# Where the maxima are transposed in the first attention: a bank of the maximum pass, ahead of the last value products

## The chip, the cores and the metric

The kernel runs on one core of a Trainium2 chip. The metric is device microseconds (us) from the first to the last instruction of the program, median of several runs. The engines of the core are TensorE (PE in the profile; its weight loads are PEld), VectorE (DVE), ScalarE (ACT), GpSimd (POOL) and SyncE (SP, which issues the DMAs here). Each executes its own list of instructions in order and waits on semaphores for the others. TensorE writes only to PSUM, which has eight banks of 512 float32 columns in 128 partitions.

## The reference

Two layers. The change is in the attention of the first one, which takes the first half of the time:

```python
b, s, d = x.shape                                  # 4, 1024, 256
q = jnp.einsum('bsd,hqd->bhsq', x, w_q)            # 16 heads of 64
k = jnp.einsum('bsd,hqd->bhsq', x, w_k)
v = jnp.einsum('bsd,hvd->bhsv', x, w_v)
scores = jnp.einsum('bhsq,bhtq->bhst', q, k)
masked = jnp.where(causal, -jnp.inf, scores)
weights = jax.nn.softmax(masked / jnp.sqrt(jnp.float32(dq)), axis=-1)
out = jnp.einsum('bhst,bhtv->bhsv', weights, v)
return jnp.einsum('bsf,df->bsd', cat, w_o)
...
x = x + _layernorm(_L0_attn_ref(_layernorm(x, axis=-1), ...), axis=-1)
x = x + _layernorm(_L0_ffn_ref(_layernorm(x, axis=-1), ...), axis=-1)   # a second attention and 8 experts, top 2
```

## The kernel before

`attention_one` works on pairs of heads: 8 pairs in each of 4 sequences, so 32 pairs. A pair goes through four steps of a pipeline, and in every step four pairs are at work: `n0` gets the first halves of its Q and K projections, `n1` the second halves, its V and its maximum pass, `n2` its scores, exponentials and value products, and `n3` its last value products, sums and normalisation.

A step has 12 slots (`n` = 0 to 11). Each slot is one unit of scores of `n2`, a block of 128 keys by up to 512 queries, for both heads `h`. The order inside a slot is written out by hand, for every engine in its own `step` function, and the engines meet through semaphores alone. The steps run in loops: an inner loop of two steps a turn (line 257), an outer loop over three sequences (line 265), and some steps written out at both ends.

- The **maximum pass** of `n1` (PE line 641) computes scores without a shift into three banks in turn, `MX[c % 3]`, 24 matmuls a pair. DVE takes the row maxima from them (lines 501 and 504), and its last instruction, line 507, writes `minus` (128 x 16), the negated maxima of both heads.
- The **turn**: PE transposes `minus` (line 726), DVE copies the result into `minusT` (line 527, function `turn`), and SP sends it by two DMAs into row 64 of `QS` (line 381). The semaphores are `minus_ready`, `turn_ready`, `turn_copied` and `minus_in`. The scores of that pair in the next step (lines 577 and 578, a product of 128 rows and one of 65 rows, the 65th holding the negated maxima) wait for `minus_in` at their first unit.
- The bank `PV` takes four things in turn: the second half of the Q projection (`qk(n1, p, 0, 1, PV)`, line 618, slot 0), V (line 626), the sums of the later half of the queries (line 605), and the transposed maxima. In the last step of a sequence (`wo` set) the output projection (line 651) uses it too, and ACT takes the rows out (`proj_copied`).
- **Slots 9, 10 and 11** of a step: in slot 9 PE projects the first half of K of `n0` into `PK`. In slot 10 ACT copies it out for both heads between its exponentials (line 407) and DVE computes the rounding rests, `split_k` (line 520). PE issues the value products of group 4 in slot 10 (`output`, line 595), which wait for the masks of POOL (line 330). In slot 11 there are only the last scores of the step.
- DVE also does the additions of head 0 for the row sums (line 291, `late_add`) and POOL those of head 1.

Below, the end of slot 10 to the start of slot 0 is called a boundary; there are 32, one for each pair, numbered from 0.

Of the kernel before, what the change touches and what calls it, by code (L numbers as in the profile page):

```python
# [16 lines left out]
P = 128  # L17
# [5 lines left out]
ST_N = S // P  # L23
# [163 lines left out]
def attention_one(nc, hold, w_pair, w_out, inv_rows):  # L187
# [5 lines left out]
    with ExitStack() as ctx:  # L193
# [278 lines left out]
        def _(dve):  # L472
# [50 lines left out]
            def turn(n1):  # L523
                dve.wait_ge(s["turn_ready"], n1 + 1)

                dve.wait_ge(s["minus_in"], n1 * 32 + 1)
                dve.tensor_copy(minusT[:, :], PV[0:2 * ST_N, 0:P]).then_inc(s["turn_copied"], 1)

            def step(n0, n1, n2, n3, p, begins=False, wo=None):
                for n in range(NU):  # L530
# [6 lines left out]
                    one_max()  # L537
                    for h in range(2):
                        if n1 is not None and n == Q1_SLOT:
                            split_q(n1, p, 1, h)  # L540
                        if n1 is not None and n == K1_SLOT + 1:
                            split_k(n1, p, 1, h)
                        if n0 is not None and n == Q0_SLOT + 1:
                            split_q(n0, 1 - p, 0, h)
                        if n0 is not None and n == K0_SLOT + 1:
                            split_k(n0, 1 - p, 0, h)
                        one_max()
                    while maxima:
                        one_max()
                    if n1 is not None and n == TURN1_SLOT:  # L550
                        turn(n1)
# [8 lines left out]
        def _(pe):  # L560
# [69 lines left out]
            def maximum(n1, p, c):  # L630
# [8 lines left out]
                pe.wait_ge(s["max_used"], n1 * NMAX + c + 1)  # L639
                bank = MX[c % MAX_BANKS1]  # L640
# [14 lines left out]
            def step(n0, n1, n2, n3, p, begins=False, wo=None):  # L655
                for n in range(NU):
# [6 lines left out]
                    if n1 is not None and n == Q1_SLOT:  # L663

                        pe.wait_ge(s["turn_copied"], n1 + 1)
                        qk(n1, p, 0, 1, PV)
# [33 lines left out]
                    one_max()  # L700
                    if n3 is not None and n == 0:
                        output(n3, p, GROUPS - 1)
# [9 lines left out]
                    if n3 is not None and n == SUM_SLOT[1]:  # L712
# [3 lines left out]
                        elif n2 is not None:  # L716
                            pe.wait_ge(s["turn_copied"], n2 + 2)
# [3 lines left out]
                    if n1 is not None and n == TURN1_SLOT:  # L721
                        pe.wait_ge(s["minus_ready"], n1 + 1)
                        pe.wait_ge(s["v_copied"], n1 * 4 + 4)
                        if wo is not None:
                            pe.wait_ge(s["proj_copied"], wo * WO_GROUPS + (WO_GROUPS + 1))
                        pe.transpose(PV[0:2 * ST_N, 0:P], minus[:, :], ident[:, :]).then_inc(s["turn_ready"], 1)
# [1235 lines left out]
```

## Time and profile before

| | |
|---|---|
| median of 3 runs | 3100.15 us (3084.71 to 3101.48) |
| profiled execution, its time | 3102.33 us |
| profiled execution, its span | 3100.0 us |
| PE busy | 2526.3 us, 81% of the span |
| DVE busy | 1577.3 us, 51% |
| ACT busy | 1475.8 us, 48% |
| POOL busy | 882.8 us, 28% |
| first attention | about 45 to 1490 us of the span |
| mean granted TensorE clock | 0.912 of full |

The profile gives for each engine when it is busy, and for idle time which engine or DMA ended it. PE is busy in nine tenths or more of nearly every fortieth of the first attention, with a granted clock of 0.9 or more there, where no other engine is busy over seven tenths. A matmul's duration overlaps the next one's, so a row of several ("x4") is the better measure. "issue" as a releaser means that nothing the profile shows held the engine.

### The profile page before, as it was taken

The page shows a single profiled execution, that of the slowest core. Times are in us where ns is not written, and L with a number is a line of the kernel's source. Part 1 is how long each engine was busy: PE and PEld are TensorE (multiplying, and loading weights), DVE is VectorE, ACT ScalarE, POOL GpSimd, SP SyncE. Part 2 cuts the span into 40 slices and gives each one's busy share as a digit, 9 for nine tenths or more (in the row PEclk, how much of TensorE's full clock was granted, in tenths as well). Part 3 has the DMA queues.
Part 4 walks back from the last instruction along what each step waited for, and adds up shares of the span by engine and source line. Part 5 has one row for each costly group of instructions (what it writes and reads, how often), then busy time and mean ns, then how long its engine had stood idle before and what let it go on. Part 6 is the DMA issues. An engine that isn't in the chain of part 4 may idle for free. (4 is left out here: it accounts for less than half of the span.)

```text
span 3100.0 us, 56250 instructions
## 1 busy us (share of the span) xinstructions
PE 2526.3 (81%) x12770; PEld 1441.6 (47%) x12771; DVE 1577.3 (51%) x3757; ACT 1475.8 (48%) x3174; POOL 882.8 (28%) x1636
## 2 busy tenths in 40 slices
PE   5999998999999999999465989888886509999950
PEld 3555565555655556554332333333334505666630
DVE  6666645666366663665476666666643302222225
ACT  3555544555355553555264666666664202222212
POOL 0244423444243442445132222222221160000035
PEclk7999999999999999999787999999999559999975
DMA  2001100101000010001233011111105422111124
GB/s 96 11 25 24 38 22 17 25 24 36 17 22 24 19 36 22 17 25 29 68 127 118 17 30 30 30 30 30 30 15 180 179 97 92 46 44 46 46 63 124
DMA packets 155681, 152.47 MB, mean 49 GB/s; under 512 B 67328, under 2 KB 127744, under 8 KB 153856
## 3 DMA queue, kind: packets, MB, share of 16 engines
q1 hardware_dynamic: 139008, 124.51, 13.0%
q0 software_dynamic: 6144, 16.79, 1.6%
q10 hardware_dynamic: 10368, 9.44, 0.9%
q8 instruction: 50, 0.82, 0.1%
q14 instruction: 111, 0.91, 0.1%
HBM read 87.76 MB, written 47.45 MB: 44 GB/s over the span
## 5 line engine op out<-in xcount | busy, mean ns | idle before, releaser
L1219 DVE TENSOR_REDUCE b_peak<-b_MX 128x1 f32<-128x512 f32 (+3 forms) x768 | 379.2, 551 | 206.4 <-PE b_MX L1306 181.6
L1175 ACT ACTIVATE b_P<-b_SC 128x512 f32<-128x512 f32 (+3 forms) x768 | 350.5, 490 | 206.2 <-PE b_SC L1252 185.5
L291 POOL TENSOR_TENSOR a_A<-a_A,a_P 128x512 f32<-128x512 f32 (+3 forms) x320 | 318.0, 994 | 308.8 <-PE a_O L595 296.1
L443 ACT ACTIVATE a_P<-a_SC 128x512 f32<-128x512 f32 (+3 forms) x640 | 293.7, 469 | 234.3 <-PE a_SC L578 200.7
L501 DVE CUSTOM_DVE_ANT_0 a_MX<-a_MX,a_causal 128x128 f32<-128x128 f32 (+3 forms) x512 | 249.9, 501 | 265.4 <-PE a_MX L641 258.0
L577 PE MATMUL a_SC<-a_QR,a_KR 128*128 128x512 f32 (+3 forms) x768 | 320.1, 421 | 15.1 <-DMA a_QS<-a_minusT 11.6
L641 PE MATMUL a_MX<-a_KR,a_QR 128*128 128x512 f32 (+3 forms) x768 | 290.0, 386 | 10.4 <-DVE a_peak L501 6.2
L1122 POOL TENSOR_SCALAR_AFFINE_SELECT b_P<-b_P 128x128 f32<-128x128 f32 x512 | 147.2, 292 | 525.5 <-ACT b_P L1175 520.5
L1252 PE MATMUL b_SC<-b_Q,b_K 98*128 98x512 bf16 (+3 forms) x768 | 250.4, 339 | 33.7 <-ACT b_P L1175 31.5
L578 PE MATMUL a_SC<-a_QS,a_KS 65*128 65x512 f32 (+3 forms) x768 | 268.4, 353 | 0.0
L1722 PE MATMUL e_GU<-W,e_hT 128*128 x576 | 260.9, 596 | 1.0 <-ACT e_hT L1774 0.8
L1303 PE MATMUL b_MX<-b_K,b_Q 96*128 96x512 bf16 (+3 forms) x768 | 238.3, 340 | 17.7 <-DVE b_peak L1219 12.0
L595 PE MATMUL a_O<-a_P,a_V 128*64 128x512 f32 (+3 forms) x1280 | 234.7, 479 | 17.3 <-POOL a_P L330 14.9
L577 PEld LDWEIGHTS a_SC<-a_QR,a_KR 128*128 128x128 f32 x768 | 148.7, 194 | 183.9 <-issue 112.1
L504 DVE TENSOR_REDUCE a_peak<-a_MX 128x1 f32<-128x512 f32 x256 | 169.7, 684 | 100.1 <-PE a_MX L641 100.0
L330 POOL TENSOR_SCALAR_AFFINE_SELECT a_P<-a_P 128x128 f32<-128x128 f32 x448 | 145.7, 334 | 233.8 <-ACT a_P L443 229.5
L291 DVE TENSOR_TENSOR a_A<-a_A,a_P 128x512 f32<-128x512 f32 (+3 forms) x320 | 199.3, 623 | 22.9 <-PE a_O L595 10.2
L618 PE MATMUL a_PK<-hold,a_W 128*128 (+1 forms) x384 | 188.7, 615 | 16.2 <-DMA a_W<-in_w_pair 6.9
L1835 POOL DMA_INDIRECT c_E<-done_rows,place x64 | 70.2, 1096 | 453.9 <-PEq L1820 434.7
L1812 DVE TENSOR_TENSOR e_gate<-e_gate,e_GU 128x512 f32<-128x512 f32 x72 | 49.5, 688 | 291.4 <-PE e_GU L1722 291.4
L641 PEld LDWEIGHTS a_MX<-a_KR,a_QR 128*128 128x128 f32 x768 | 147.5, 192 | 69.5 <-DVE a_peak L501 33.5
L443 ACT ACTIVATE a_A<-a_SC 128x512 f32<-128x512 f32 x128 | 76.6, 599 | 210.0 <-PE a_SC L578 209.3
(240 smaller groups left out, 4162.3 us busy)
## 6 DMA issues: line engine op xcount, KB each, us to landing
a_inv<-inv_rows SPq DMA_DIRECT2D x128, 128.0 KB, 3.0
stack_rows<-p_stk SPq DMA_DIRECT2D x32, 480.0 KB, 2.6
a_W<-in_w_pair SPq DMA_DIRECT2D x34, 384.0 KB, 3.5
b_stk<-stack_rows SPq DMA_DIRECT2D x136, 96.0 KB, 2.0
e_G<-sorted_rows SPq DMA_DIRECT2D x74, 128.0 KB, 2.0
sorted_rows<-r_zeros SPq DMA_DIRECT2D x6, 1536.0 KB, 5.9
done_rows<-e_out ACTq DMA_DIRECT2D x72, 128.0 KB, 1.7
W<-in_w SPq DMA_DIRECT2D x8, 1024.0 KB, 11.7
```

The lines of the kernel that those rows point to most:

```text
L291: eng.tensor_tensor(acc[h][c][:, a:], acc[h][c][:, a:], buffer(n, h)[:, a:], ALU.add).then_inc(added[h], 1)
L443: act.activation(buffer(n, h)[:, a:], SC[h][:, a:], ACT.Exp, scale=DH1 ** -0.5).then_inc(s["exp_done"], 1)
L501: dve.tensor_tensor_reduce(MX[c % MAX_BANKS1][:, 0:w], MX[c % MAX_BANKS1][:, 0:w], causal[:, BANK - w:], 1.0, 3 * NEG, ALU.add, ALU.max, p ...
L577: pe.matmul(SC[h][:, a:], KR[p][h][:, keys], QR[p][h][:, queries], start=True, stop=False)
L578: pe.matmul(SC[h][:, a:], KS[p][h][:, keys], QS[p][h][:, queries], start=False, stop=True).then_inc(s["scores_ready"], 1)
L595: pe.matmul(O[DH1 * h:DH1 * (h + 1), a:], V[p][h][:, j, :], buffer(n, h)[:, a:], start=(j == 0), stop=(n in LAST)).then_inc(s["pv_done"], 1)
L641: pe.matmul(bank[:, 0:w], QR[p][h][:, i * P:(i + 1) * P], KR[p][h][:, ch * BANK:ch * BANK + w], start=True, stop=True).then_inc(s["max_rea ...
L1175: act.activation(probs[k % RING2][:, a:], SC[k % SCORE_BANKS][:, a:], ACT.Exp, scale=DH2 ** -0.5).then_inc(s["exp_done"], 1)
L1219: dve.tensor_reduce(peak[:, h, i, ch:ch + 1], MX[n % MAX_BANKS][:, 0:w], AX.X, ALU.max).then_inc(s["max_used"], 1)
L1252: pe.matmul(SC[k % SCORE_BANKS][:, a:], K[p2][:, j * P:(j + 1) * P], Q[p2][:, h, c * BANK + a:(c + 1) * BANK], start=True, stop=True).then ...
L1303: last = pe.matmul(MX[n % MAX_BANKS][:, 0:w], Q[p][0:STACK, h, i * P:(i + 1) * P], K[p][0:STACK, ch * BANK:ch * BANK + w], start=True, sto ...
L1722: last = pe.matmul(GU[i][half][:, :], hT[i][:, kt, :], W13[:, bass.ds(e, 1), kt, half * FFN:(half + 1) * FFN].rearrange("p a f -> p (a f)" ...
```

## The change

The transpose of `minus` goes into `MX[NMAX % MAX_BANKS1]`. `NMAX` is 24 and `MAX_BANKS1` is 3, so that is `MX[0]`, the bank that the maximum pass of the next pair uses first. It stands in slot 10 ahead of the value products instead of behind them, and DVE's copy stands ahead of `split_k` instead of behind it. The Q projection of slot 0 no longer waits for that copy; it waits for V having been taken out of `PV`, and for the rows of the output projection. The first matmul of the next maximum pass waits for the copy instead.

```diff
@@ DVE, turn and step @@
-                dve.tensor_copy(minusT[:, :], PV[0:2 * ST_N, 0:P]).then_inc(s["turn_copied"], 1)
+                dve.tensor_copy(minusT[:, :], MX[NMAX % MAX_BANKS1][0:2 * ST_N, 0:P]).then_inc(s["turn_copied"], 1)
...
                     one_max()
+                    if n1 is not None and n == TURN1_SLOT:
+                        turn(n1)
                     for h in range(2):
...
-                    if n1 is not None and n == TURN1_SLOT:
-                        turn(n1)
@@ PE, maximum @@
                 pe.wait_ge(s["max_used"], n1 * NMAX + c + 1)
+                if c == NMAX % MAX_BANKS1:
+                    pe.wait_ge(s["turn_copied"], n1 + 1)
@@ PE, step @@
                     if n1 is not None and n == Q1_SLOT:
-                        pe.wait_ge(s["turn_copied"], n1 + 1)
+                        if n2 is not None:
+                            pe.wait_ge(s["v_copied"], n2 * 4 + 4)
+                        if not isinstance(n1, int) or n1 >= 2:
+                            pe.wait_ge(s["proj_copied"], (n1 - 2) // PAIRS * WO_GROUPS + 1)
                         qk(n1, p, 0, 1, PV)
...
                     one_max()
+                    if n1 is not None and n == TURN1_SLOT:
+                        pe.wait_ge(s["minus_ready"], n1 + 1)
+                        pe.transpose(MX[NMAX % MAX_BANKS1][0:2 * ST_N, 0:P], minus[:, :], ident[:, :]).then_inc(s["turn_ready"], 1)
                     if n3 is not None and n == 0:
                         output(n3, p, GROUPS - 1)
                     if n2 is not None and n in PV_SLOT:
                         output(n2, 1 - p, PV_SLOT[n])
...
                         elif n2 is not None:
-                            pe.wait_ge(s["turn_copied"], n2 + 2)
+                            pe.wait_ge(s["v_copied"], n2 * 4 + 4)
                         sums(n3, 1)
...
-                    if n1 is not None and n == TURN1_SLOT:
-                        pe.wait_ge(s["minus_ready"], n1 + 1)
-                        pe.wait_ge(s["v_copied"], n1 * 4 + 4)
-                        if wo is not None:
-                            pe.wait_ge(s["proj_copied"], wo * WO_GROUPS + (WO_GROUPS + 1))
-                        pe.transpose(PV[0:2 * ST_N, 0:P], minus[:, :], ident[:, :]).then_inc(s["turn_ready"], 1)
```

The order on PE from slot 10 to the next step's slot 0, first of before, in the inner loop. L595 are the value products, L726 the transpose, L577 and L578 the scores of slot 11, L618 the Q projection.

```order
359 L595 MATMUL a_O<-a_P,a_V 64x512 [waits a_exp_done]
360 L595 MATMUL a_O<-a_P,a_V 64x512
361 L595 MATMUL a_O<-a_P,a_V 64x384 x2
362 L722 ISA
363 L723 ISA [waits a_minus_ready]
364 L726 MATMUL a_PV<-a_ident,a_minus 16x128 [waits a_v_copied]
365 L576 ISA
366 L577 MATMUL a_SC<-a_QR,a_KR 128x128 [waits a_exp_done]
```

And of the change, the same place, where the transpose is line 709:

```order
356 L578 MATMUL a_SC<-a_QS,a_KS 128x256
357 L708 ISA
358 L709 MATMUL a_MX<-a_ident,a_minus 16x128 [waits a_minus_ready]
359 L589 ISA
360 L589 ISA [waits a_masked]
361 L590 ISA [waits a_masked]
362 L595 MATMUL a_O<-a_P,a_V 64x512 [waits a_exp_done]
```

The transpose has moved from behind the four value products of slot 10 to directly behind that slot's scores, ahead of the wait for the masks.

The order on DVE in slot 10 of before. L291 is an addition, L520 is `split_k`, L527 the copy, L492 the reciprocal of the sums.

```order
285 L291 TENSOR_TENSOR a_A<-a_A,a_P 128x512 [waits a_added0]
286 L519 ISA
287 L520 TENSOR_TENSOR a_KR<-a_PK,a_KR 64x512 [waits a_k_copied]
288 L519 ISA
289 L520 TENSOR_TENSOR a_KR<-a_PK,a_KR 64x512 [waits a_k_copied]
290 L524 ISA
291 L526 ISA [waits a_turn_ready]
292 L527 CAST a_minusT<-a_PV 16x128 [waits a_minus_in]
```

And of the change:

```order
285 L291 TENSOR_TENSOR a_A<-a_A,a_P 128x512 [waits a_added0]
286 L524 ISA
287 L526 ISA [waits a_turn_ready]
288 L527 CAST a_minusT<-a_MX 16x128 [waits a_minus_in]
289 L519 ISA
290 L520 TENSOR_TENSOR a_KR<-a_PK,a_KR 64x512 [waits a_k_copied]
291 L519 ISA
292 L520 TENSOR_TENSOR a_KR<-a_PK,a_KR 64x512 [waits a_k_copied]
```

The copy has moved past the two `split_k`, and stands behind the addition of slot 9 as they did.

## Rows read from the trace of the kernel before

**Rows 1.** Stretches: from:to, length, busy us of each engine, granted clock, DMA

```profile
90.00:1440.00 1350.00, 1252.07 (x5817) 753.07 (x5818) 777.70 (x1903) 718.33 (x1481) 527.50 (x854) 0.97 0.09 24
604.00:613.00 9.00, 6.42 (x26) 2.82 (x24) 4.88 (x10) 3.31 (x9) 6.48 (x10) 1.00 0.02 1
613.00:645.00 32.00, 31.24 (x154) 19.09 (x154) 20.80 (x54) 19.98 (x40) 10.10 (x18) 1.00 0.13 29
```

**Rows 2.** Groups by line, 90 to 1440 us: busy, mean ns, idle before, releasers

```profile
L577 PE MATMUL a_SC<-a_QR,a_KR 128*128 128x384 f32 (+1 forms) x736 | 305.9, 419 | 11.8 <-DMA a_QS<-a_minusT 9.1 <-ACT a_A L443 0.9
...
L595 PE MATMUL a_O<-a_P,a_V 128*64 128x384 f32 (+1 forms) x1224 | 223.5, 478 | 15.6 <-POOL a_P L330 13.2 <-ACT a_P L443 2.2
...
L618 PE MATMUL a_PV<-hold,a_W 128*128 (+1 forms) x120 | 78.1, 786 | 47.3 <-DVE a_minusT L527 39.1 <-issue 8.2
```

**Rows 3.** Timeline of boundary 12: start, duration, instruction, idle before and releaser

```profile
604.37 0.19 DVE L507 TENSOR_REDUCE a_minus<-a_peak 128x16 f32<-128x32 f32 x1
...
604.82 0.70 DVE L291 TENSOR_TENSOR a_A<-a_A,a_P 128x512 f32<-128x512 f32 x1 [0.27 <-issue]
...
605.51 1.72 PE L595 MATMUL a_O<-a_P,a_V 128*64 128x512 f32 x8
...
607.16 0.28 PE L726 MATMUL a_PV<-a_ident,a_minus 128*16 128x128 f32 x1
...
607.57 0.28 PE L578 MATMUL a_SC<-a_QS,a_KS 65*128 65x128 f32 x1
...
608.62 0.69 DVE L520 TENSOR_TENSOR a_KR<-a_PK,a_KR 64x512 fp32r<-64x512 f32 x1 [0.82 <-ACT a_KS L407]
...
609.34 0.28 DVE L527 CAST a_minusT<-a_PV 16x128 fp32r<-16x128 f32 x1
...
610.00 1.98 PE L618 MATMUL a_PV<-hold,a_W 128*128 x4 [2.15 <-DVE a_minusT L527]
...
612.41 0.50 PE L577 MATMUL a_SC<-a_QR,a_KR 128*128 128x512 f32 x1 [0.43 <-DMA a_QS<-a_minusT]
...
613.75 0.30 DVE L501 CUSTOM_DVE_ANT_0 a_MX<-a_MX,a_causal 128x128 f32<-128x128 f32 x1 [2.05 <-PE a_MX L641]
```

**Rows 4.** Timeline of boundary 13, where PE waits for a mask first

```profile
645.01 0.19 DVE L507 TENSOR_REDUCE a_minus<-a_peak 128x16 f32<-128x32 f32 x1
...
647.58 1.72 PE L595 MATMUL a_O<-a_P,a_V 128*64 128x512 f32 x8 [1.36 <-POOL a_P L330]
```

**Rows 5.** Timeline of boundaries 14 and 15: the reduces, and the Q projection of 14

```profile
685.65 0.19 DVE L507 TENSOR_REDUCE a_minus<-a_peak 128x16 f32<-128x32 f32 x1
...
691.29 3.68 PE L618 MATMUL a_PV<-hold,a_W 128*128 x4 [1.76 <-DVE a_minusT L527]
...
727.31 0.19 DVE L507 TENSOR_REDUCE a_minus<-a_peak 128x16 f32<-128x32 f32 x1
```

**Rows 6.** Stretches of 8 us behind the transposes of boundaries 12 and 14

```profile
607.86:615.86 8.00, 5.22 (x21) 2.71 (x22) 4.12 (x9) 3.57 (x9) 3.60 (x6) 1.00 0.19 24
...
689.56:697.56 8.00, 6.27 (x22) 3.49 (x22) 3.52 (x8) 2.73 (x7) 3.19 (x5) 0.79 0.10 28
```

**Rows 7.** PE's branches back in the inner loop: ns min/median/max, first and last start us

```profile
L257 PEldq COMPARE_BRANCH  x11: 76/216/241, 203.7 to 1367.2; - x11
```

**Rows 8.** PE's branches back in the outer loop, the same columns

```profile
L265 PEldq COMPARE_BRANCH  x3: 79/3446/3732, 481.1 to 1204.1; - x3
```

**Rows 9.** Timeline of boundary 17, behind the outer loop's branch back

```profile
847.15 2.07 PE L618 MATMUL a_PV<-hold,a_W 128*128 x2 [3.87 <-issue]
```

**Rows 10.** Timeline of boundary 0: the transpose and the first scores

```profile
80.77 0.27 PE L726 MATMUL a_PV<-a_ident,a_minus 128*16 128x128 f32 x1
...
87.16 0.82 PE L577 MATMUL a_SC<-a_QR,a_KR 128*128 128x512 f32 x1
```

**Rows 11.** Timeline of boundary 31: the addition behind the maxima, the first scores

```profile
1441.85 1.45 DVE L291 TENSOR_TENSOR a_A<-a_A,a_P 128x512 f32<-128x512 f32 x1
...
1446.48 0.80 PE L577 MATMUL a_SC<-a_QR,a_KR 128*128 128x512 f32 x1 [2.53 <-DMA a_QS<-a_minusT]
```

## The prediction, written before the changed kernel was timed

> **What bounds the kernel now.** I read the busy times by stretch first, then the groups of instructions by line, then the timeline of single boundaries. Between 90 and 1440 us TensorE is busy 1252 of 1350 us, DVE 778, ACT 718 and POOL 528 [rows 1]: this stage is TensorE's. But its idle time is not spread evenly. In the 9 us around boundary 12 it is busy 6.42 us, in the 32 us behind it 31.24 [rows 1]. So a step (some 40.6 us) has one hole. The groups name it: the Q projection waits 39.1 us for DVE's copy of the transposed maxima in 27 boundaries, and the first scores 9.1 us for the DMA that carries them; the value products wait 13.2 us for POOL's masks and 2.2 for ACT [rows 2].
>
> The timeline of boundary 12 says why. I count from the end of the last reduce, 604.37 + 0.19 = 604.56. The value products start at +0.95, the transpose at +2.60, and the last scores of the step end at 607.85, +3.29. DVE's copy could follow the transpose, but it stands behind two `split_k`, which wait for ACT's copies of K; the second runs from 608.62 to 609.31. The copy runs from +4.78 to +5.06, the Q projection starts at +5.44 after 2.15 us of idle time, and the first scores at 612.41, +7.85, after 0.43 us more [rows 3]. When POOL is late the hole only changes its place: in boundary 13 the value products wait 1.36 us [rows 4]. So the chain reduce, ACT's K, `split_k`, copy, Q projection, DMA sets the step, and a late mask is hidden in it.
>
> **The change, part by part.**
>
> *Copy ahead of `split_k`.* The new chain: the scores of slot 10 are through on TensorE about when the value products start, +0.95, so the transpose is there too. DVE's addition, now directly ahead of the copy, ends at 605.52, +0.96 [rows 3]. I put the copy at +1.3 to +1.6. From the end of the copy (609.62) to the first scores (612.41) the two DMAs take 2.79 us [rows 3], so the maxima are in place at +4.4. The copy's 0.28 us only move, and the two `split_k`, which wait for ACT, start when they did. The transpose itself costs nothing that it didn't cost before; where the masks are late it fills idle time.
>
> *No wait in front of the Q projection.* V was taken out of `PV` slots before, so the waits that replace it are met. The projection can start when the last scores end, +3.29. What is left is the engine's own work on registers, which the old wait hid in part: from the copy's end to the projection 0.38 us pass now [rows 3], so the price is between 0 and 0.4 us, plus 0.22 us for the branch at every second boundary [rows 7]. I take 0.25. The projection (1.98 us) then ends at about +5.5, and the first scores find the maxima there since +4.4. They start at +5.5 instead of +7.85: 2.35 us a boundary, if no mask is late.
>
> *Over all.* A mask that is late keeps its wait, so I sum the idle time that goes: 39.1 + 9.1 = 48.2 us [rows 2], less 27 x 0.25 = 6.8, is 41.4. Boundary 0 has no value products: transpose at 80.77, copy about 0.3 later for 0.28, maxima in place 2.79 later at 84.15, against 87.16 now [rows 10]: 3.0. In boundary 31 the addition behind the reduce, 1441.85 to 1443.30, holds DVE, so the copy comes hardly earlier and the scores at 1446.48 gain 0.3 [rows 11]. In two boundaries TensorE waits 3.4 to 3.7 us for its outer loop's branch back [rows 8, 9], and nothing is to be gained there (8.2 us of "issue" in [rows 2] with one small wait). Sum: 41.4 + 3.0 + 0.3 = 44.7 us.
>
> On that branch the Trainium skill ("Runtime: NRT & Kernel Launch", section on instruction fetch mechanics) says that a taken branch whose target isn't in the window of the instruction memory forces a fetch before execution goes on. The trace agrees for the outer loop (3446 ns) and not for TensorE's inner one (216 ns).
>
> *The clock.* In the 8 us behind boundary 12's transpose the granted clock is 1.00, behind that of 14 it is 0.79, which is 3.4 us at 1.2 instead of 2.4 GHz [rows 6]. It falls where TensorE has just been idle: the Q projection behind 1.76 us of idle time takes 3.68 us instead of 1.98 [rows 5, 3]. Of the seven ordinary boundaries among eight that I looked at in a row, three are so, hence some 12 of 29. The price: reduce to reduce it is 727.31 - 685.65 = 41.66 us against 645.01 - 604.37 = 40.64 [rows 3 to 5], so 1.02; and such a boundary has no 0.43 us wait for the DMA, which is thus lost too: 1.45. If all went, that gave 17 us, if none, 0. The waits for masks, up to 1.4 us, stay in half of the boundaries, so I take three quarters, 9 x 1.45 = 13 us.
>
> *The wait added to the first maximum.* It is met at +1.6; that matmul stands behind the first scores, +5.5. It also needs both `split_k`, done at 609.31, +4.75. DVE waits 2.05 us for its product now and is free from 611.70 [rows 3]; with TensorE 2.35 us earlier DVE may be 0.3 us late, which the three banks cover: nothing, at most 27 x 0.3 = 8 us. *Removed waits of the transpose* (V, rows of the output projection): always met, nothing.
>
> Together 44.7 + 13 = 58 us. The profiled execution took 3102.33 us (2.2 above the median of the runs), so it would take 3044, and I forecast that for the median as well.
>
> **Rivals.**
>
> *Masks take over* (12%). The late masks (15 us in sum [rows 2]) were hidden by a chain that ended at +4.78 whether they were late or not; now each counts in full. If POOL, whose work is not shortened, fell behind by 1 us more in each step, 27 us of the 44.7 were lost and about half of the 13: 3078. For: POOL is busy 6.48 of the 9 us at a boundary. Against: it is busy 10.1 of the 32 us between [rows 1], so what it is behind by should not add up.
>
> *The DMA of the maxima becomes the end* (8%). Its slack is 1.1 us. If the copy waited for a longer addition (boundary 31's takes 1.45 us instead of 0.70 [rows 11, 3]) and SP came late, the first scores would start up to 0.8 us later: 27 x 0.8 = 22 us, 3066.
>
> *Branches of the other engines* (6%). Their inner loops branch back 7 times, and the waits for TensorE might hide fetches there. At 3.4 us like TensorE's outer one, those 7 boundaries would gain nothing: 16 us less, 3060. Against: TensorE's inner branch costs 0.22 us [rows 7]. The Trainium skill's rule above would have it so: the same section gives the engines other than TensorE a smaller instruction memory. No row here shows their fetches.
>
> *K is the true bound* (3%). If the first maximum's wait for `split_k` just replaced the old one, nothing would change: 3101. It has 1.5 us of slack.
>
> *Slower: TensorE stops for the maxima ahead of the value products* (2%). The transpose now stands in front of them, so a late reduce holds everything behind it: value products, last scores, Q projection. The reduce ends at 0 and TensorE arrives shortly before +0.95, so DVE has about 0.8 us. Only from about 3.1 us later does it cost more than the 2.35 won; at 4.2 us, TensorE would stand 3.4 us, 1.05 us net in 28 boundaries, 3130. Against: DVE waits for TensorE, not the reverse [rows 3].
>
> **How the numbers follow.** The forecast has 69%; its own range is 3030 (no halved clock, no register price: 48.2 + 3.3 + 17 = 69 us, 3034, and some run-to-run spread) to 3060 (no clock gained, 44.7 us, 3058). For 8 in 10 I go down to 3026, since one of the three runs was 15 us under the median, and up to 3070, which takes in the branches and the DMA. Half a per cent, 16 us, is about what a measurement can tell from no change. Faster by more: all cases but the last two, less a little for the first rival turning out worse, 0.93; within it 0.05; slower 0.02.
>
> **What would show it.** Right: the Q projection's idle time before it falls from 47.3 us to about 15, with no wait for the copy; the first scores wait under 2 us for the DMA; the copy stands 1.3 us behind the reduce; reduce to reduce 38.3 us where no mask is late; fewer boundaries under 1.00. The wait of the value products stays near 15 us. Wrong: the first scores wait for the DMA in most boundaries; the value products' wait over 30 us; a long wait of the transpose for line 507; or a granted clock in this stage that is no higher than 0.97.

## The result and the profile after

| | before | changed |
|---|---|---|
| median of the runs | 3100.19 us (3084.71 to 3101.48) | 3020.53 us (3017.6 to 3022.14) |
| profiled execution, its time | 3102.33 us | 3020.58 us |
| profiled execution, its span | 3100.0 us | 3018.0 us |

The change takes 2.5% off: the ratio is 0.9751, with a 95% interval of 0.9735 to 0.9767. The forecast of 3044 us was 23.5 us too high, and the result lies 5.5 us below the range of 3026 to 3070. The direction and the mechanism were right; the size of the clock's term was not.

The stage between the reduce of boundary 0 and that of boundary 31 is what moved. Line 507 on DVE, first of before and then of the changed kernel, start, duration, instruction:

```profile
80.41 0.19 DVE L507 TENSOR_REDUCE a_minus<-a_peak 128x16 f32<-128x32 f32 x1
...
1441.75 0.19 DVE L507 TENSOR_REDUCE a_minus<-a_peak 128x16 f32<-128x32 f32 x1
```

```profile
80.16 0.19 DVE L507 TENSOR_REDUCE a_minus<-a_peak 128x16 f32<-128x32 f32 x1
...
1361.82 0.19 DVE L507 TENSOR_REDUCE a_minus<-a_peak 128x16 f32<-128x32 f32 x1
```

1361.34 us became 1281.66, 79.7 less, which is nearly all of the 81.75 us between the two profiled executions. The stretches of the changed kernel (from:to, length, busy us of PE, PEld, DVE, ACT, POOL, granted clock, DMA share, GB/s), against [rows 1] and [rows 6]; the last two are the 8 us behind the transposes of boundaries 12 and 14:

```profile
90.00:1362.00 1272.00, 1219.25 (x5816) 741.07 (x5814) 770.40 (x1903) 717.70 (x1480) 533.30 (x854) 0.99 0.10 26
570.00:579.00 9.00, 8.69 (x38) 4.83 (x38) 6.17 (x13) 5.02 (x12) 7.61 (x14) 1.00 0.02 1
579.00:610.00 31.00, 30.11 (x148) 17.96 (x145) 20.79 (x55) 19.20 (x39) 10.78 (x19) 1.00 0.12 30
572.72:580.72 8.00, 7.57 (x38) 4.05 (x36) 5.03 (x11) 5.68 (x13) 5.20 (x9) 1.00 0.10 15
649.42:657.42 8.00, 7.54 (x38) 4.01 (x36) 4.99 (x11) 5.64 (x13) 5.17 (x8) 1.00 0.03 3
```

The hole of boundary 12 is closed: 8.69 of 9 us busy instead of 6.42. The number of PE's instructions is the same (5816 against 5817), so the two stretches hold the same work, and the gain splits into two parts: idle time fell from 1350 - 1252.07 = 97.9 us to 1272 - 1219.25 = 52.8, 45.1 less, and **busy time fell too**, from 1252.07 to 1219.25, 32.8 less. Most of that goes with the clock: 0.99 instead of 0.97 over the whole stretch, and 1.00 instead of 0.79 behind boundary 14. Counted in the trace from the first to the last reduce, the kernel before has 22 stretches of 3.4 us with the clock at 1.2 GHz (75.1 us), the changed one 6 (20.5 us), two each behind boundaries 9, 17 and 27.

The groups by line, 90 to 1362 us (busy us, mean ns, idle before them, releasers), against [rows 2]:

```profile
L577 PE MATMUL a_SC<-a_QR,a_KR 128*128 128x256 f32 (+1 forms) x738 | 307.3, 420 | 2.6
L644 PE MATMUL a_MX<-a_KR,a_QR 128*128 128x384 f32 x738 | 279.1, 385 | 11.0 <-DVE a_peak L501 9.2
...
L595 PE MATMUL a_O<-a_P,a_V 128*64 128x384 f32 (+1 forms) x1224 | 222.1, 475 | 8.4 <-POOL a_P L330 4.9 <-ACT a_P L443 3.5
...
L618 PE MATMUL a_PV<-hold,a_W 128*128 (+1 forms) x120 | 62.2, 643 | 11.7 <-issue 11.6
```

The Q projection (L618) waits for no copy any more, and its idle time went from 47.3 to 11.7 us, its busy time from 78.1 to 62.2. The first scores (L577) lost 9.2 us of idle time, the value products (L595) 7.2. Two groups have more: the maximum pass 11.0 us instead of 6.8 (9.2 of them for DVE), and the projections into `PK` 8.1 instead of 6.0.

Boundary 12 after the change, start, duration, instruction, idle before it; [rows 3] is its partner:

```profile
571.66 0.19 DVE L507 TENSOR_REDUCE a_minus<-a_peak 128x16 f32<-128x32 f32 x1
...
572.12 0.69 DVE L291 TENSOR_TENSOR a_A<-a_A,a_P 128x512 f32<-128x512 f32 x1 [0.27 <-issue]
...
572.72 0.27 PE L709 MATMUL a_MX<-a_ident,a_minus 128*16 128x128 f32 x1
...
572.92 1.73 PE L595 MATMUL a_O<-a_P,a_V 128*64 128x512 f32 x8
...
573.25 0.28 DVE L527 CAST a_minusT<-a_MX 16x128 fp32r<-16x128 f32 x1 [0.44 <-PE a_MX L709]
...
575.55 1.98 PE L618 MATMUL a_PV<-hold,a_W 128*128 x4 [0.31 <-issue]
...
575.92 0.69 DVE L520 TENSOR_TENSOR a_KR<-a_PK,a_KR 64x512 fp32r<-64x512 f32 x1 [0.82 <-ACT a_KS L407]
...
576.97 0.79 PE L577 MATMUL a_SC<-a_QR,a_KR 128*128 128x512 f32 x1
```

The reduce ends at 571.85. The transpose stands at +0.87, the copy at +1.40 to +1.68, the Q projection at +3.70 (before: +5.44), and the first scores at +5.12 behind it, without idle time (before: +7.85). Boundary 13, where POOL is late as in [rows 4], and the reduce of 14:

```profile
609.86 0.19 DVE L507 TENSOR_REDUCE a_minus<-a_peak 128x16 f32<-128x32 f32 x1
...
611.92 1.73 PE L595 MATMUL a_O<-a_P,a_V 128*64 128x512 f32 x8 [0.74 <-POOL a_P L330]
...
614.08 1.94 PE L618 MATMUL a_PV<-hold,a_W 128*128 x4
...
648.37 0.19 DVE L507 TENSOR_REDUCE a_minus<-a_peak 128x16 f32<-128x32 f32 x1
```

The step that ends with boundary 13 took 38.20 us, and 38.51 the one behind it, with the late mask. Before, both took 40.64 [rows 3 to 5].

### The profile page after: what moved, and what is told of

Its sections match the earlier page's. It is cut to its first block and busy times, and to the rows that moved or that the text cites. A ratio compares the mean times of both kernels' runs of the same rounds, so it can differ in the third digit from the quotient of the medians.

```text
span 3018.0 us, 56282 instructions
## 1 busy us (share of the span) xinstructions
PE 2493.1 (83%) x12770; PEld 1428.6 (47%) x12771; DVE 1572.7 (52%) x3757; ACT 1476.6 (49%) x3174; POOL 889.2 (29%) x1636
## 5 line engine op out<-in xcount | busy, mean ns | idle before, releaser
L291 POOL TENSOR_TENSOR a_A<-a_A,a_P 128x512 f32<-128x512 f32 (+3 forms) x320 | 321.4, 1004 | 303.7 <-PE a_O L595 291.0
L577 PE MATMUL a_SC<-a_QR,a_KR 128*128 128x512 f32 (+3 forms) x768 | 319.8, 420 | 7.3 <-DMA a_QS<-a_minusT 2.9
L644 PE MATMUL a_MX<-a_KR,a_QR 128*128 128x512 f32 (+3 forms) x768 | 290.0, 386 | 14.8 <-DVE a_peak L501 11.3
L578 PE MATMUL a_SC<-a_QS,a_KS 65*128 65x512 f32 (+3 forms) x768 | 265.5, 350 | 0.0
L595 PE MATMUL a_O<-a_P,a_V 128*64 128x512 f32 (+3 forms) x1280 | 232.7, 476 | 10.1 <-POOL a_P L330 6.6
L577 PEld LDWEIGHTS a_SC<-a_QR,a_KR 128*128 128x128 f32 x768 | 146.0, 190 | 182.8 <-issue 93.4
L291 DVE TENSOR_TENSOR a_A<-a_A,a_P 128x512 f32<-128x512 f32 (+3 forms) x320 | 194.8, 609 | 21.5 <-PE a_O L595 9.0
L618 PE MATMUL a_PK<-hold,a_W 128*128 (+1 forms) x384 | 188.7, 614 | 18.2 <-issue 8.1
L1269 PE MATMUL b_O<-b_P,b_V 128*32 128x512 f32 (+3 forms) x1536 | 166.5, 507 | 0.1
## 6 DMA issues: line engine op xcount, KB each, us to landing
W<-in_w SPq DMA_DIRECT2D x8, 1024.0 KB, 11.6
```

The source lines that it names most:

```text
L291: eng.tensor_tensor(acc[h][c][:, a:], acc[h][c][:, a:], buffer(n, h)[:, a:], ALU.add).then_inc(added[h], 1)
L577: pe.matmul(SC[h][:, a:], KR[p][h][:, keys], QR[p][h][:, queries], start=True, stop=False)
L578: pe.matmul(SC[h][:, a:], KS[p][h][:, keys], QS[p][h][:, queries], start=False, stop=True).then_inc(s["scores_ready"], 1)
L595: pe.matmul(O[DH1 * h:DH1 * (h + 1), a:], V[p][h][:, j, :], buffer(n, h)[:, a:], start=(j == 0), stop=(n in LAST)).then_inc(s["pv_done"], 1)
L644: pe.matmul(bank[:, 0:w], QR[p][h][:, i * P:(i + 1) * P], KR[p][h][:, ch * BANK:ch * BANK + w], start=True, stop=True).then_inc(s["max_rea ...
```

## The experiments

My theory: the copy behind `split_k` and the wait for it made the hole; the parts add up; and short idle time at a boundary brings the halved clock with it. The rivals: it is one of the parts alone; or the clock has nothing to do with it; or what the changed kernel has left is the late masks, or register work and branches.

Ratios are to the kernel before on the same chip; its median was 3093 to 3100 us in these comparisons.

**The copy alone.** Before, with DVE's copy ahead of `split_k`; the transpose stays in `PV`, and the Q projection keeps its wait.

```diff
@@ DVE, step @@
                     one_max()
+                    if n1 is not None and n == TURN1_SLOT:
+                        turn(n1)
                     for h in range(2):
...
-                    if n1 is not None and n == TURN1_SLOT:
-                        turn(n1)
```

> The kernel before with one part of the change: DVE's copy of the transposed maxima ahead of the two split_k. The transpose stays in PV, behind the value products, and the Q projection still waits for the copy. Theory 1 (the copy was late because it stood behind split_k, and that chain set the step): without a late mask the copy ends at +3.5 instead of +5.06 from the end of the last reduce, the Q projection starts at +3.9 and the first scores at +6.3 instead of +7.85. That is 1.5 us a boundary, less wherever a mask is late (15 us in sum), so 27 x 1.5 - 15 = 25 us, and about half of the clock: 3060 to 3070 us. Theory 2 (the position of the transpose and the other bank bring the gain, not DVE's order): 3095 to 3100 us.

Measured: 3054.25 us (3053.9 to 3065.45), ratio 0.9877 (0.9845 to 0.9909). Half of the gain, and 6 us more than expected. The groups, 90 to 1440 us (this window, and that of the groups in the next experiments, reaches to the end of the stage or past it):

```profile
L577 PE MATMUL a_SC<-a_QR,a_KR 128*128 128x256 f32 (+1 forms) x764 | 309.5, 409 | 19.8 <-DMA a_QS<-a_minusT 17.5 <-ACT a_P L443 0.7
...
L618 PE MATMUL a_PV<-hold,a_W 128*128 (+1 forms) x120 | 62.6, 646 | 18.7 <-DVE a_minusT L527 10.1 <-issue 8.2
```

With `split_k` out of the copy's way, the Q projection waits only 10.1 us for it. But the transpose is still behind the value products, and so the maxima come late: 17.5 us of waits for the DMA.

**The copy put back.** The changed kernel, with the copy behind `split_k` again (the same four lines the other way round).

> The changed kernel without its part on DVE: the transpose goes early into MX[0] and the Q projection doesn't wait for the copy, but the copy stands behind both split_k as before. Theory 1: the maxima are in place at +7.85 as before, so the idle time only moves from the Q projection to the first scores, about 2.3 us a boundary with the DMA as its releaser: 3090 to 3102 us. Theory 2 (the freed Q projection is what counts): most of the gain stays, 3020 to 3045 us.

Measured: 3097.28 us (3091.22 to 3098.83), ratio 1.0004 (0.9993 to 1.0015). The whole gain is gone, although the Q projection doesn't wait for the copy and the transpose is early:

```profile
L577 PE MATMUL a_SC<-a_QR,a_KR 128*128 128x384 f32 (+1 forms) x739 | 308.2, 421 | 58.5 <-DMA a_QS<-a_minusT 56.8
...
L618 PE MATMUL a_PV<-hold,a_W 128*128 (+1 forms) x120 | 62.2, 643 | 11.1 <-issue 11.0
```

```profile
90.00:1360.00 1270.00, 1181.72 (x5469) 721.87 (x5469) 729.07 (x1781) 677.21 (x1389) 488.36 (x795) 0.96 0.09 24
```

Between 90 and 1360 us TensorE is idle for 88.3 us, against 92.9 before in the same stretch. The idle time has only moved behind the Q projection, to the first scores. DVE's order is the necessary part: without it the other two bring nothing.

**The transpose late.** The changed kernel, with its transpose behind the value products, where it was, but still in `MX[0]`.

```diff
@@ PE, step @@
                     one_max()
-                    if n1 is not None and n == TURN1_SLOT:
-                        pe.wait_ge(s["minus_ready"], n1 + 1)
-                        pe.transpose(MX[NMAX % MAX_BANKS1][0:2 * ST_N, 0:P], minus[:, :], ident[:, :]).then_inc(s["turn_ready"], 1)
                     if n3 is not None and n == 0:
...
                     while maxima:
                         one_max()
+                    if n1 is not None and n == TURN1_SLOT:
+                        pe.wait_ge(s["minus_ready"], n1 + 1)
+                        pe.transpose(MX[NMAX % MAX_BANKS1][0:2 * ST_N, 0:P], minus[:, :], ident[:, :]).then_inc(s["turn_ready"], 1)
```

> The changed kernel with its transpose behind the value products, where it was before; bank, waits and DVE's order as changed. Theory 1: the copy comes at +2.9 at the earliest, the maxima are there at about +6.3, and the first scores wait some 0.8 us for the DMA in nearly every boundary: 27 x 0.8 = 22 us, 3035 to 3050 us. Theory 2 (the place ahead of the value products buys nothing, the DMA has slack): 3018 to 3024 us.

Measured: 3056.88 us (3049.53 to 3060.46), ratio 0.9873 (0.9842 to 0.9904).

```profile
L577 PE MATMUL a_SC<-a_QR,a_KR 128*128 128x256 f32 (+1 forms) x764 | 309.9, 409 | 31.7 <-DMA a_QS<-a_minusT 29.1 <-ACT a_P L443 0.9
```

So the place ahead of the value products is worth 36 us; I had expected 15 to 30. It is the same ratio as with the copy alone: the free Q projection is worth nothing as long as the transpose is late, because the first scores wait for the DMA instead.

**The wait put back.** The changed kernel, with the Q projection waiting for both `split_k`, which is when the old copy came.

```diff
@@ PE, step, slot Q1_SLOT @@
                             pe.wait_ge(s["proj_copied"], (n1 - 2) // PAIRS * WO_GROUPS + 1)
+                        k_used(n1, 0)
                         qk(n1, p, 0, 1, PV)
```

> The changed kernel with one wait put back into its old place: ahead of the Q projection TensorE waits until both split_k are done (+4.75 from the end of the last reduce). The maxima still travel early. That opens a hole of some 1.6 us in 27 boundaries, 43 us. If only the idle time counts: 3060 to 3066 us. If TensorE's clock falls in such holes again, each stretch at half clock adds 1.7 us, since TensorE is now what sets the step: with 10 to 20 of them 3075 to 3095 us.

Measured: 3065.07 us (3062.18 to 3065.21), ratio 0.9898 (0.9879 to 0.9917).

```profile
L618 PE MATMUL a_PV<-hold,a_W 128*128 (+1 forms) x124 | 69.8, 691 | 47.1 <-DVE a_KR L520 37.6 <-issue 9.4
```

```profile
90.00:1360.00 1270.00, 1187.86 (x5585) 721.44 (x5584) 741.53 (x1823) 690.36 (x1424) 508.37 (x822) 0.99 0.10 25
```

The Q projection's idle time is back at its old size (47.3 us in [rows 2]), 35.4 more than in the changed kernel. The kernel is 44.5 us slower than that one. Most of the other 9 us are the clock: 11 stretches at 1.2 GHz instead of 6 (37.5 us instead of 20.5), thus 8.5 us of lost work. An ordinary step takes 39.6 us without such a stretch here and 40.9 to 41.2 with one. The time lies in the range that I had given for idle time alone, but the clock has its part in it. The three parts of the change are links of one chain: each one put back takes 36 to 77 of the 80 us away, so their worth can't be added.

**The clock by itself.** Before, with five matmuls more, whose result nothing uses, between the last scores and the Q projection's wait. The engine is then busy where it was idle, and the wait for the copy is unchanged.

```diff
@@ PE, step @@
                     if n1 is not None and n == Q1_SLOT:
+                        if n2 is not None:
+                            for _ in range(5):
+                                pe.matmul(MX[1][:, :], KR[1 - p][0][:, 0:P], QR[1 - p][0][:, 0:BANK], start=True, stop=True)
                         pe.wait_ge(s["turn_copied"], n1 + 1)
```

> The kernel before with five more matmuls of 512 columns (some 1.2 us of TensorE, their product is never read) ahead of the Q projection's wait for the copy. No dependency is changed and the step's chain is as long as before; only TensorE is busy in most of the hole. Clock theory (some 30 of the 80 us came from TensorE's clock, which falls where it was idle): stretches at half clock at the boundaries go, 12 to 16 of them at 1.0 to 1.7 us each: 3075 to 3088 us. Rival (the gain over the forecast has another source, such as POOL's masks): 3098 to 3106 us, whatever the clock does.

Measured: 3087.92 us (3084.02 to 3094.94), ratio 0.9981 (0.9966 to 0.9996). Its stretch from 90 to 1360 us, the group of the added matmuls (90 to 1440 us) and its first and last reduce:

```profile
90.00:1360.00 1270.00, 1202.07 (x5669) 726.77 (x5670) 737.45 (x1807) 683.99 (x1410) 500.94 (x814) 1.00 0.10 25
```

```profile
L667 PE MATMUL a_MX<-a_QR,a_KR 128*128 128x512 f32 x150 | 41.5, 406 | 7.1 <-issue 7.1
```

```profile
79.22 0.19 DVE L507 TENSOR_REDUCE a_minus<-a_peak 128x16 f32<-128x32 f32 x1
...
1422.85 0.18 DVE L507 TENSOR_REDUCE a_minus<-a_peak 128x16 f32<-128x32 f32 x1
```

150 matmuls more, 41.5 us of work, and the kernel is not slower. The granted clock is 1.00 in the whole stretch, 1 stretch at 1.2 GHz is left of 22, and first to last reduce takes 1343.63 us instead of 1361.34, 17.7 less. That is what the halved clock cost in the old chain: 17.7 / 21 = 0.8 us a stretch, although PE lost 1.7 us of work in each (3.4 us at half speed); the rest was hidden in the chain over K. By the medians the kernel gains only 5.7 us, since the number of such stretches differs from run to run: the mean granted clock of the kernel before lies between 0.911 and 0.921, that of the profiled execution is 0.912. Over the 39 runs of the kernel before in these comparisons its time rises by 0.79 us with every 3.4 us at half clock (an estimate, fitted to their times and clocks), which is the same price. So the link between the idle time and the clock is shown, and in the traces the forecast's 13 us for the clock was below even this.

**The late masks.** In the changed kernel POOL normalises the second half of `n3` in slot 9 instead of slot 7, except in the last step of a sequence, so that it is free when the masks of slot 10 are due.

```diff
@@ POOL, step @@
                     for k in range(2):
-                        if n3 is not None and n == NORM_SLOT[k]:
+                        if n3 is not None and n == (9 if k == 1 and wo is None else NORM_SLOT[k]):
                             normalise_out(n3, k)
```

> The changed kernel with POOL's normalisation of the later half moved from slot 7 behind the masks and addition of slot 9, except in the steps with an output projection, so that no mask is late for the value products of slot 10. If a late mask counts in full, as the prediction had it, the 10 us that the value products wait for masks or exponentials go: 3009 to 3013 us. If most of it is paid back (the registers of the Q projection are worked out meanwhile, and the transpose fills the wait), 2 to 5 us go: 3015 to 3019 us.

Measured: 3019.2 us (3017.71 to 3022.07), ratio 0.9751 (0.9733 to 0.9769), which is that of the changed kernel. The groups, 90 to 1440 us:

```profile
L595 PE MATMUL a_O<-a_P,a_V 128*64 128x512 f32 (+3 forms) x1280 | 233.3, 477 | 3.7 <-POOL a_P L330 3.5
...
L618 PE MATMUL a_PV<-hold,a_W 128*128 (+1 forms) x120 | 62.5, 645 | 16.7 <-issue 16.7
```

and boundary 13, where POOL was late:

```profile
609.71 0.19 DVE L507 TENSOR_REDUCE a_minus<-a_peak 128x16 f32<-128x32 f32 x1
...
613.89 1.98 PE L618 MATMUL a_PV<-hold,a_W 128*128 x4 [0.61 <-issue]
...
648.20 0.19 DVE L507 TENSOR_REDUCE a_minus<-a_peak 128x16 f32<-128x32 f32 x1
```

The masks come in time, and hardly anything is won. Of the value products' 8.4 us of idle time 0.3 are left (in the same stretch of work, x1224), but the Q projection waits 5.0 us more ("issue", 11.7 us before, 16.7 now). The rest is lost to the clock here: 7 stretches at 1.2 GHz instead of 6. First to last reduce is 1281.29 us instead of 1281.66. In the changed kernel boundary 13 has its wait for the mask and no gap before the Q projection; here it has a gap of 0.61 us and no wait. The step is 38.49 us against 38.51. The registers of the Q projection are prepared while PE's queue stands at the mask, so the two are not added; the longer one counts. This run also shows what a stretch at 1.2 GHz costs where TensorE sets the pace: the step behind boundary 8 has one and takes 61.85 us, the same step of the next sequence, behind boundary 16, has none and takes 60.17, 1.7 less.

The same edit on the kernel before:

> The kernel before with POOL's normalisation of the later half moved behind the masks of slot 9, as in the last experiment on the changed kernel. The late masks of slot 10 (15 us in sum) should go. If they were hidden in the chain over split_k, as the prediction said: no change, within 4 us of the kernel before. If they counted there: 8 to 15 us less.

Measured: 3104.05 us (3098.24 to 3110.4), ratio 1.0024 (1.0014 to 1.0035).

```profile
L595 PE MATMUL a_O<-a_P,a_V 128*64 128x384 f32 (+1 forms) x1224 | 222.1, 475 | 0.1
...
L618 PE MATMUL a_PV<-hold,a_W 128*128 (+1 forms) x120 | 82.4, 825 | 64.4 <-DVE a_minusT L527 56.2 <-issue 8.2
```

The 15.5 us that the value products no longer wait come back as 17.1 us before the Q projection, and its first to last reduce is 1361.00 us, as before. This shows what the forecast said of the old chain: a late mask is hidden in it. The kernel is nevertheless some 8 us slower, all of it in the second attention, 690.5 us against 682.4, where the edit changes nothing. The second attention of the kernel before, and of this one:

```profile
1658.50:2341.00 682.50, 590.11 (x4369) 247.58 (x4369) 410.36 (x884) 435.52 (x882) 152.74 (x533) 0.96 0.11 30
```

```profile
1658.90:2349.40 690.50, 601.71 (x4368) 253.28 (x4368) 411.33 (x883) 436.32 (x882) 153.75 (x533) 0.93 0.11 30
```

The same matmuls are busy for 11.6 us more at a granted clock of 0.93 instead of 0.96: 96.6 us at 1.2 GHz instead of 61.2. Why the clock fell more often there stays open.

**Loops.** One boundary of the changed kernel got worse: the step behind boundary 27 took 44.1 us, against 42.75 before. Its first maxima:

```profile
1218.13 0.30 DVE L501 CUSTOM_DVE_ANT_0 a_MX<-a_MX,a_causal 128x128 f32<-128x128 f32 x1 [3.66 <-issue]
...
1220.56 0.08 DVE L501 DVE_READ_ACCUMULATOR2_ANT a_peak<- 128x1 f32 x1 [2.13 <-issue]
1220.70 0.79 PE L644 MATMUL a_MX<-a_KR,a_QR 128*128 128x512 f32 x1 [4.99 <-DVE a_peak L501]
```

DVE has its branch back at 1213.3 us and its next instruction at 1217.8, in the last inner loop alone; PE runs out of banks and waits 4.99 us. The kernel before had this too, hidden in its waits: branch back at 1288.3 us, next instruction at 1291.2. The test: the changed kernel, with the last inner loop written out.

```diff
-            steps(N - PAIRS, PAIRS // 2 - 2)
+            steps(N - PAIRS, PAIRS // 2 - 2, unrolled=True)
```

> The changed kernel with the last inner loop (4 steps of the last sequence) written out instead of looped. Theory: the 5.0 us that TensorE waits for DVE behind that loop's branch back, and the half clock that follows, are a fetch of instructions: 6 to 7 us less, 3013 to 3015 us. Rival (DVE is late for another reason, or straight code fetches as long): 3019 to 3022 us.

Measured: 3014.07 us (3012.89 to 3015.54), ratio 0.9737 (0.9719 to 0.9755): 6.5 us less. That alone would hardly stand out of the spread, but the trace shows it at the place itself: the step behind boundary 27 takes 37.1 us instead of 44.1, and has no such wait.

With the outer loop written out too (`with eng.Fori(0, B - 1) as b:` becomes `for b in range(B - 1):`):

> As the one before, and the outer loop over three sequences written out too (the inner loops of three turns stay). Theory: the two branches back of the outer loop cost 4.2 to 4.5 us of idle time each and two stretches at half clock behind it, which boundary 25, without a branch, doesn't have: 51.4 against 44.3 us from reduce to reduce, so 14 us less than the last kernel: 2999 to 3001 us. Rival (longer code pays in other fetches): 3010 to 3020 us.

Measured: 2977.36 us (2976.08 to 2981.42), ratio 0.9616 (0.9599 to 0.9634), the **best version** of this study, 120 us under the kernel before on the same chip (3097.19), and 22 us under what I had expected. The Q projection's group, and the reduces of boundaries 12 and 13:

```profile
L624 PE MATMUL a_PV<-hold,a_W 128*128 128x512 f32 x120 | 58.0, 606 | 0.0
```

```profile
558.13 0.19 DVE L513 TENSOR_REDUCE a_minus<-a_peak 128x16 f32<-128x32 f32 x1
...
595.31 0.19 DVE L513 TENSOR_REDUCE a_minus<-a_peak 128x16 f32<-128x32 f32 x1
```

I had counted only the outer loop's branches (the steps behind boundaries 9 and 17 went from 51.4 and 51.2 to 44.1 us). But an ordinary step fell too, from 38.20 to 37.18 us between boundaries 12 and 13. With constants in place of most registers (the three inner loops are still loops) the "issue" gap in front of the Q projection, 11.7 us in sum, some 8 of them the two branches, is 0.0, and so is that of the projections into `PK`, 8.1 us in the changed kernel. The stage has no stretch at 1.2 GHz any more. The masks later as well, in this kernel:

> The changed kernel with the outer and the last inner loop written out (2977 us) and POOL's normalisation moved behind the masks of slot 9. There the Q projection has constant addresses, no work on registers is left to hide a late mask, and TensorE waits 3.2 us in sum for masks: 2973 to 2977 us if they count in full, 2976 to 2979 if not.

Measured: 2980.09 us (2978.53 to 2981.67), ratio 0.9617 (0.9601 to 0.9633). By the medians that is no change, but 3 us, all that could be won, are less than they can tell. The traces can: first to last reduce takes 1239.91 us instead of 1243.19. The value products of boundary 2, with the loops written out and then with the masks later too:

```profile
155.33 1.73 PE L601 MATMUL a_O<-a_P,a_V 128*64 128x512 f32 x8 [1.02 <-POOL a_P L336]
```

```profile
154.71 1.73 PE L601 MATMUL a_O<-a_P,a_V 128*64 128x512 f32 x8
```

Without the late mask the step behind boundary 2 takes 37.18 us instead of 38.28, and the next one 37.30 instead of 38.32. So once most of the register work is gone a late mask counts in full in these two steps, as the prediction had it; in the loops most of it didn't. And the kernel before, with the same loops written out:

> The kernel before with the outer and the last inner loop written out, nothing else: what the change is worth without work on registers. The chain over split_k stays as long: only the 0.3 us between copy and Q projection (27 times, 8 us) and the two branches back of the outer loop (14 us) go: 3070 to 3076 us, so that the change would then be worth some 95 us instead of 76. Rival: the work on registers held TensorE in this kernel as much as in the changed one, 1 us a step: 3055 to 3062 us.

Measured: 3064.09 us (3061.95 to 3066.91), ratio 0.9893 (0.9877 to 0.991).

```profile
L583 PE MATMUL a_SC<-a_QR,a_KR 128*128 128x384 f32 (+1 forms) x766 | 309.7, 408 | 22.6 <-DMA a_QS<-a_minusT 21.5 <-ACT a_P L449 0.7 <-ACT a_A L449 0.3
...
L624 PE MATMUL a_PV<-hold,a_W 128*128 128x512 f32 x120 | 60.3, 625 | 44.3 <-DVE a_minusT L533 44.3
```

That lies between the two forecasts, 3070 to 3076 us and 3055 to 3062. With these loops written out the change is worth 3064.09 - 2977.36 = 87 us by medians from two chips, and 1320.01 - 1243.19 = 76.8 us from first to last reduce, against 80 and 79.7 in the loops: about the same. The old chain (44.3 us of waits for the copy, 21.5 for the DMA) is there with loops or without, and hides part of what unrolling brings an ordinary step: 40.64 us became 39.93 between boundaries 12 and 13, 0.7 less, where the changed kernel won 1.0. The halved clock is nearly gone from this kernel too (3 stretches instead of 22), although TensorE is still idle for 81 us between 90 and 1360 us, 93 before.

## Why the prediction was right, and where it was wrong

**The chain and its times: right.** The copy was put at +1.3 to +1.6 and stands at +1.40 to +1.68. The Q projection was forecast at the end of the last scores plus 0.25 us, and has 0.31 us of "issue" before it. A step with masks in time was to gain 2.35 us; from boundary 12 to 13 it gains 40.64 - 38.20 = 2.44, and the mean of the sixteen steps that had no halved clock before is 2.28.

**The DMA is not the end: right.** It has no wait worth naming in the stage (2.6 us before L577, all causes). The wait of the first maximum costs nothing at ordinary boundaries.

**Ends: right.** Boundary 0 and boundary 31:

```profile
83.83 0.50 PE L577 MATMUL a_SC<-a_QR,a_KR 128*128 128x512 f32 x1 [1.32 <-DMA a_QS<-a_minusT]
...
1366.18 0.50 PE L577 MATMUL a_SC<-a_QR,a_KR 128*128 128x512 f32 x1 [1.60 <-DMA a_QS<-a_minusT]
```

The first scores of boundary 0 come 3.3 us earlier than in [rows 10], 3.1 of them behind the reduce (forecast 3.0). Those of 31 come 1366.18 - 1362.01 = 4.17 us behind the reduce's end, 4.54 before [rows 11]: 0.37, forecast 0.3. And the two boundaries behind the outer loop's branch gained nothing, as said.

**"If all went, that gave 17 us ... I take three quarters, 9 x 1.45 = 13 us": wrong, and the largest part of the miss.** This is the term that was mis-sized; what the clock gave back was 26 us. Three things in it failed. The count: I found three of seven ordinary boundaries and made 12 of them, but the steps with the output projection have such stretches too; there were 22. What goes: I let a quarter stay for the sake of the late masks, but from 10 to 16, for instance, all ordinary boundaries are at 1.00; 16 of the 22 went. The price: 1.45 us was 1.02 us of step time and 0.43 us of a wait for the DMA that the slow work had filled. The filled old kernel shows 0.8 us of step time. But beside a sum of idle time a stretch has to stand with all the work that it lost, 3.4 us at half speed, 1.7, and in the changed kernel, where TensorE sets the pace, that is also what it costs in time (61.85 against 60.17 us, above). 16 x 1.7 = 27 us instead of 13. The trace agrees: from 90 us on TensorE was busy for 66.9 us at 1.2 GHz before, and for 14.8 after; half of the difference is 26 us.

Busy time fell by 32.8 us, though, 7 more than that. Added up line by line it fell by 25.4 only (1670.5 to 1645.1 us, the PE groups of the two stretches); the other 7.4 us are matmuls of different lines whose times overlap more in the changed kernel. The profile models the ends of matmuls, so this part is rough, and the forecast had no term for it.

**"A mask that is late keeps its wait": wrong.** The sum left 15.4 us of masks and 27 x 0.25 = 6.8 us of register work in place, as if they added up. In the changed kernel the value products' idle time is 8.4 us, and that of the Q projection beyond the branches' 8.2 is 3.5: 11.9 instead of 22.2. First, less of the wait is left: 0.74 us of boundary 13's 1.36. Of these 0.6 us the transpose, which now runs inside the wait, fills only 0.1; the masks themselves come 0.5 us earlier, the value products at +1.87 instead of +2.38 behind the reduce. Second, the register work goes on behind what is left, which taking the masks away showed (hardly anything won in the loops, 1.0 to 1.1 us in each of two steps once they were written out). The step behind boundary 13 gained 2.13 us, where my own working gave 2.35 - 1.36 = 0.99.

**What went the other way.** The maximum pass waits 11.0 us instead of 6.8, 4.99 of it in one place: DVE's branch of the last inner loop. That is the rival "branches of the other engines", and it is true of one boundary out of the seven that I had counted; it costs 6.5 to 7 us, not 16. The rule of the Trainium skill ("Runtime: NRT & Kernel Launch", section on instruction fetch mechanics), that a taken branch out of the window of the instruction memory forces a fetch, fits that branch (4.5 us) and the outer loop's on PE. TensorE's short inner branch (216 ns) doesn't speak against it, as my prediction had it, since the rule is about targets outside the window alone. That the time is a fetch isn't shown; that it goes with the loop is. PE's branch back of the outer loop in the changed kernel:

```profile
L265 PEldq COMPARE_BRANCH  x3: 79/3645/3885, 453.0 to 1135.7; - x3
```

These idle terms partly cancel: the forecast's idle time between 90 us and the end of the stage was 41.4 us, the measured one 45.1. Behind that stand two errors against each other, 10 us too little for masks and registers, and no term for DVE's branch and the other waits of the maximum pass and of the projections into `PK` (6 us together). That the idle time came out so near is luck in part. What was missed is the busy time, 32.8 us where 13 were forecast: 13 us in the clock's term and 7 in the overlap.

**The other rivals.** Masks as the new bound: no, without them the time is the same in the loops. K as the true bound: no; `split_k` begins as before behind ACT, at 575.92, and nobody waits for it. TensorE stopped for the maxima ahead of the value products: no; line 709 has no idle time before it.

## What to carry over

Where one copy waits in an in-order queue behind work that another engine feeds, look at what stands ahead of it before anything else: here the order on DVE was worth half of the gain alone, and the rest was worth nothing without it. Price a halved clock by who sets the pace: below one microsecond a stretch when another engine's chain hides it, the full lost work once TensorE does, and count such stretches over the whole stage, not in a sample of one kind of step. Beside a sum of idle time, always put the full lost work. Waits, register work and small operations in front of the same engine overlap, so take the longest, not the sum, and expect the next one to count once it is gone.

## What the runs showed of the hardware

- Idle time of the same length brings a different number of halved stretches depending on where it stands. With the copy put back, PE was idle for 1270 - 1181.72 = 88.3 us between 90 and 1360 us, and before, in the same stretch, for 1270 - 1177.15 = 92.9; but there were 33 stretches of 1.2 GHz (112.6 us) instead of 22. With the loops of the kernel before written out it was idle for 1270 - 1188.82 = 81.2 us and had 3. The runs don't show why.
- One branch back of DVE, in the last inner loop, took 4.5 us (1213.3 to 1217.8 us), and 2.9 in the kernel before; in the other inner loops its next instruction follows within 0.4 us.
- Register work for addresses is invisible as long as the engine waits for others, and cost 1.0 us of a step of 38.2 once it didn't.
- The second attention took 682 us in both kernels of the comparison, but 690.5 and 688.5 us in two others (masks later in the kernel before; the loops written out), which don't touch it. It goes with the clock, as counted in the traces: 96.6 and 77.6 us at 1.2 GHz there, 61.2 and 68.0 in the pair. Why the clock differs is open; it means that the best version loses some 6 us there.
